# A two-layer adaLN kernel on one core: where the attention's bulk transfers and head 0's first loads stand in the queues

## The reference

```python
q = (xn @ Wq.T + bq).reshape(b, t, h, dh)
k = (xn @ Wk.T + bk).reshape(b, t, h, dh)
v = (xn @ Wv.T + bv).reshape(b, t, h, dh)
p = (pos_emb @ Wpos.T).reshape(2 * t - 1, h, dh)
content_score = jnp.einsum('bthd,bshd->bhts', q + u_bias, k)
pos_score = jnp.einsum('bthd,phd->bhtp', q + v_bias, p)
pos_score = _rel_shift(pos_score)
score = (content_score + pos_score) / math.sqrt(dh)
attn = jax.nn.softmax(score, axis=-1)
```

## Time and profile before

| | us |
|---|---|
| median of 3 runs (1020.45 to 1026.05) | 1023.15 |
| profiled execution, device time | 1029.01 |
| its span, first to last instruction | 1027.1 |
| mean granted TensorE clock | 0.917 of full |

### The profile page before, as it was taken

How to read it: one execution, slowest core, us unless ns; L and a number is a source line. 1 busy time by engine, 2 the same in 40 slices (tenths; PEclk the granted TensorE clock), 3 DMA queues, 4 the chain that set the end, 5 groups by cost and what they waited for, 6 DMA issues and landing times.

```text
span 1027.1 us, 23784 instructions
## 1 busy us (share of the span) xinstructions
PE 828.7 (81%) x9611; PEld 602.8 (59%) x9611; DVE 719.5 (70%) x1458; ACT 538.3 (52%) x985; POOL 413.7 (40%) x476
## 2 busy tenths in 40 slices
PE   2493799999999999975479998999998785257773
PEld 1252577878788888764256655666665474135563
DVE  5974656555555555425778898788786688899994
ACT  3860456677667675445545556566564644313332
POOL 5444533443344334344433245344343127214444
PEclk9986699999999999986589999999999798569998
DMA  9037613333333323541000000000000000000111
GB/s 136 11 65 215 174 39 75 94 82 78 73 92 86 79 69 85 149 97 34 1 1 2 2 1 1 2 1 2 1 2 1 1 1 1 0 1 11 20 23 31
DMA packets 55289, 47.17 MB, mean 46 GB/s; under 512 B 22259, under 2 KB 44987, under 8 KB 54459
## 3 DMA queue, kind: packets, MB, share of 16 engines
q1 hardware_dynamic: 36176, 26.23, 11.1%
q0 software_dynamic: 8416, 18.85, 7.3%
q10 hardware_dynamic: 10587, 0.57, 0.7%
HBM read 30.52 MB, written 12.06 MB: 41 GB/s over the span
## 4 chain that ended last, share of the span: by engine, by line
PE 53%; DVE 27%; issue 4%; DMA 4%; POOL 4%; ACT 4%; SPq 3%; POOLq 0%; DVEq 0%; ACTq 0%
PE PS L1154 12%; PE PS L1271 6%; PE PS L1272 5%; PE PS L1273 5%; PE PS L1127 5%; PE PS L1158 5%; PE PS L1176 5%; PE PS L1129 3%; DVE HB L1948 2%; DVE XX L1554 2%; DVE XX L1560 2%; DVE AM L1545 2%; DVE ACC L1940 1%; DVE HQ L2077 1%; DVE HN L1534 1%
## 5 line engine op out<-in xcount | busy, mean ns | idle before, releaser
L1686 DVE TENSOR_REDUCE MX<-PS 128x4 f32<-128x1024 f32 x128 | 156.4, 1224 | 120.5 <-PE PS L1129 120.1
L853 ACT ACTIVATE REG<-PS 128x1024 f32<-128x1024 f32 x128 | 130.4, 1019 | 118.4 <-PE PS L1158 112.4
L1154 PE MATMUL PS<-XX,TB 96*128 96x64 f16 x2048 | 161.3, 247 | 4.6 <-issue 2.7
L673 POOL TENSOR_TENSOR HH<-HB,HH 128x512 f16<-128x512 f32 x64 | 75.6, 1182 | 173.9 <-ACT HH L904 173.9
L1154 PEld LDWEIGHTS PS<-XX,TB 96*128 96x128 f16 x2048 | 121.9, 120 | 33.9 <-issue 12.2
L934 ACT ACTIVATE SG<-PS 128x512 f32<-128x512 f32 x128 | 76.2, 595 | 112.0 <-PE PS L1273 111.7
L1948 DVE SCALAR_TENSOR_TENSOR HB<-PS,SG 128x512 f32<-128x512 f32 x128 | 87.4, 683 | 46.0 <-ACT SG L934 46.0
L1158 PE MATMUL PS<-XX,KC 97*128 97x128 f16 x1024 | 107.8, 229 | 0.0
L1271 PE MATMUL PS<-XH,XX 128*128 128x512 f16 x256 | 98.9, 386 | 9.9 <-DVE HB L1948 9.5
L1127 PE MATMUL PS<-TM,YY 64*64 64x256 f16 x1024 | 81.5, 334 | 21.8 <-DVE YY L1728 16.3
L1272 PE MATMUL PS<-XH,XX 128*128 128x512 f16 x256 | 98.4, 384 | 0.0
(11 more groups left out here) (240 smaller groups left out, 1725.0 us busy)
## 6 DMA issues: line engine op xcount, KB each, us to landing
REG<-inverse_sums POOLq DMA_DIRECT2D x60, 128.0 KB, 2.9
KC<-keys_strips SPq DMA_DIRECT2D x16, 192.0 KB
keys_strips<-REG POOLq DMA_DIRECT2D x12, 224.0 KB, 7.2
R<-in_L_attn_x SPq DMA_DIRECT2D x32, 64.0 KB, 4.3
XX<-NEG ACTq DMA_DIRECT2D x128, 1.0 KB, 2.3
R<-REG POOLq DMA_DIRECT2D x60, 32.0 KB, 2.9
queries_position<-REG POOLq DMA_DIRECT2D x2, 896.0 KB, 8.7
XX<-queries_position SPq DMA_DIRECT2D x56, 32.0 KB
```

Of the source, the lines that this page charges most:

```text
L853: A(P[jt][:, 1024 * up:1024 * up + 1024].rearrange("p (k x) -> p k x", k=2), ST[u % 2], ACT.Exp).then_inc(exp_done, 1)
L1154: mm(o_pos[:, a], TB[p][0:96, y0:y0 + 128], xp[0:96, 8 * bank + a], start=(a == 0), stop=False, skip_group_check=True)
L1686: nc.vector.tensor_reduce(MX[h % 2][:, :].rearrange("p (r a) -> p r a", r=2)[:, :, 2 * g:2 * g + 2], PS[:, bank:bank + 2, :].rearrange("p ...
```

## The change

It moves transfers and waits in three queues; no computation is added or removed.

- **Bulk of the keys at once.** POOL's 13 bulk key transfers wait for `stage` at 14 instead of for the first heads' key transfers to have landed (`khi_first`, `k_first`).
- **SP's first transfers.** The high position queries of heads 0 to 2 (`qvb_d`) go between head 0's and head 1's key strips; before, they went behind both. Head 0's dense position queries go ahead of its key operands `KC`.
- **Dense content queries of head 0 ahead of its rows.** Its 12 position-query transfers go behind the dense content queries; before, six went ahead of them.
- `maximum_keys(1)` goes behind head 1's dense queries.
- **Bulk of the position queries later.** POOL issues `qv_d` behind its widening for head 1 and waits also for head 0's first shift row (`neg_in[0]` at 64).
- `content_first` becomes a list of two semaphores; only the second is used.

```diff
@@ SP @@
+            def first_keys(h):
+                for k, part in enumerate((0, 0, 1)):
+                    sp.dma_start(k4_d[h, :, k].rearrange("w d x -> d w x"),
+                                 NAT[NAT_K + part][DH * h:DH * h + DH, :].rearrange("p (w x) -> p w x", w=4)).then_inc(k_first, 16)
             sp.wait_ge(high_done, 14)
             sp.dma_start(khi_d[first, :], NAT[NAT_K][first, :]).then_inc(khi_first, 16)
             sp.wait_ge(stage, 14)
-            for h in range(2):
-                for k, part in enumerate((0, 0, 1)):
-                    sp.dma_start(k4_d[h, :, k].rearrange("w d x -> d w x"),
-                                 NAT[NAT_K + part][DH * h:DH * h + DH, :].rearrange("p (w x) -> p w x", w=4)).then_inc(k_first, 16)
+            first_keys(0)
             sp.wait_ge(batched, 8)
             sp.dma_start(qvb_d[first, :], NQB[first, :]).then_inc(qvb_first, 16)
+            first_keys(1)
             sp.wait_ge(khi_first, 16)
             maximum_keys(0)
+            sp.wait_ge(qvb_first, 16)
+            dense_position_queries(0)
             sp.wait_ge(k_first, 16 * 6)
             key_operands(0)
-            sp.wait_ge(qvb_first, 16)
-            dense_position_queries(0)
-            sp.wait_ge(stage, 16)
-            first_position_queries(0, range(2))
             sp.wait_ge(qu_first, 16)
             dense_content_queries(0)
-            first_position_queries(0, range(2, 4))
-            maximum_keys(1)
+            first_position_queries(0, range(4))
             dense_position_queries(1)
             dense_content_queries(1)
+            maximum_keys(1)
             key_operands(1)
@@ POOL @@
-            gp.wait_ge(khi_first, 16)
-            gp.wait_ge(k_first, 16 * 6)
+            gp.wait_ge(stage, 14)
             gp.dma_start(khi_d[rest, :], NAT[NAT_K][rest, :]).then_inc(khi_out, 16)
...
-            gp.wait_ge(x_in[0], X_FIRST[0])
-            for part in range(2):
-                gp.dma_start(qv_d[2:H, part], NAT[NAT_QV + part][2 * DH:128, :]).then_inc(qv_out, 16)
             gp.wait_ge(y_dense[1], Y_FIRST[1])
...
+            gp.wait_ge(x_in[0], X_FIRST[0])
+            gp.wait_ge(neg_in[0], 64)
+            for part in range(2):
+                gp.dma_start(qv_d[2:H, part], NAT[NAT_QV + part][2 * DH:128, :]).then_inc(qv_out, 16)
```

More of the change, by code:

```diff
@@ L260, in adaln_program @@
         l_feat, stored_last = sem("l_feat"), sem("stored_last")
-        t_evac_dve, batched, content_first, position_dense = (sem(s) for s in ("t_evac_dve", "batched", "content_first", "position_dense"))
+        t_evac_dve, batched, position_dense = (sem(s) for s in ("t_evac_dve", "batched", "position_dense"))
+        content_first = [sem(f"content_first{h}") for h in range(2)]
         block = outer.enter_context(nc.Block())
@@ L594, in _, with first_content_queries @@
                                  OWN[:, j:j + 2].unsqueeze(2).to_broadcast([128, 2, T]), ALU.mult).then_inc(y_wide[1], 1)
[L595 to L599, removed]
+            gp.wait_ge(x_in[0], X_FIRST[0])
+            gp.wait_ge(neg_in[0], 64)
+            for part in range(2):
+                gp.dma_start(qv_d[2:H, part], NAT[NAT_QV + part][2 * DH:128, :]).then_inc(qv_out, 16)
+            def first_content_queries(h):
+                for w in range(4):
+                    for k, part in enumerate(PARTS):
+                        to = 24 * w + 8 * k
+                        gp.dma_start(XC[h][to:to + 8, 1024 * w:1024 * w + 1024],
+                                     NAT[NAT_QU + part][DH * h:DH * h + DH, 1024 * w:1024 * w + 1024]).then_inc(content_first[h], 16)
+            first_content_queries(1)
             for part, h in ((0, FIRST), (1, 2)):
@@ L1141, in scores @@
                     elif h == 1:
-                        pe.wait_ge(content_first, 16 * 12)
+                        pe.wait_ge(content_first[1], 16 * 12)
                 elif h == 0 and k == 2:
```

## The result

The changed kernel took 1033.28 us (median of 4 runs, 1030.99 to 1034.53) against 1021.8 us (median of 4) for the kernel before in the same comparison. The ratio is 1.0071, with a 95% interval of 1.0037 to 1.0105: slower by 3.8 to 10.7 us. The two medians alone would give 1.0112; why the ratio is smaller is not shown, but in the three later sets the kernel before has medians of 1025.58 to 1026.03 over 24 to 29 runs, and against those 1033.28 is 1.0071 to 1.0075. The forecast was 1015, faster. A second set of runs of the same kernel, further down, gave 1.0084 (1.0054 to 1.0115).

A forecast was written before the change was run, and what follows sets the result against it. TensorE was taken as the bound, 81% busy, with a 16.27 us hole before head 0's first maximum. Gains of 6.4 and 2.3 us made 8.7, capped at 8.5 by head 1's widening: 1023.15 to 1015 us, range 1010 to 1022.

The forecast's parts named there:

- The queries' bulk: POOL's bulk of position queries: issued at 106.1 us instead of 97.34, landing at 114.8 or 115.4, at no cost.
- Some 6 us of cover remain: ACT's exponential waiting for the queries' bulk: bulk lands by about 115, exponential runs about 121.3, so no stop.
- SP's chain: SP's queue up to head 0's dense content load: issued at 82.5 us, 7.5 us earlier than 89.98.
- forecast first maximum: Head 0's first maximum on TensorE: at 90.7 us instead of 97.08, a gain of 6.4 (bounds 8.4 and 1.3).
- The 8.1: Landing time in us of head 0's old dense position load under the keys' bulk, taken for the new one.
- Rival 2: The keys' bulk starves SP's chain: first maximum at 95.8 us, a gain of 1.3; time 1019 to 1022; chance 0.26.
- arbitration rule: DMA engines alternate between queue rows by packet, so SP loads under the bulk stay near low bounds: first maximum 88.7.
- POOL's start of the keys' bulk: POOL's queue: the bulk of the keys starts at 69.14 us instead of 76.42, 7.3 us earlier.
- the shift row's gain: Ahead of the first score tile: the 2.73 us wait shrinks to about 0.4, 2.3 us gained (bounds 0 and 2.7).
- the covered row transfers: Head 0's 12 row transfers on SP: end at 94.5 us, needed at 102.0, so covered by the maxima.
- the limit set by head 1's widening: POOL's widening for head 1: ends at 106.1 us, capping the gain at 8.5 us (cap 12.6 to 5.6).
- Rival 5: TensorE's clock stays low over the rest of head 0 and head 1: costs 13 us, time 1028; chance 0.06.

The follow-up runs named there:

- e3: Changed kernel with the position queries' bulk waiting also for the second half of head 0's shift row; 0.9978 of the kernel before.
- e4: Kernel before with only the position queries' bulk moved, behind the widening and the first half of head 0's shift row; 1.0114 of the kernel before.
- e9: Kernel before with only the position queries' bulk moved, behind the widening and both halves of head 0's shift row; 0.9981 of the kernel before.
- e1: Changed kernel with the position queries' bulk back ahead of POOL's widening, waiting for head 0's rows alone; 1.0015 of the kernel before.
- e2: Changed kernel with the keys' bulk waiting for the first heads' keys again; 0.9944 of the kernel before.
- e5: Kernel before with only the keys' bulk issued at once; 1.0041 of the kernel before.
- e7: Changed kernel with the keys' bulk waiting as before and the queries' bulk behind both halves of the shift row; 0.9924 of the kernel before.
- e10: e7 with head 1's dense loads put ahead of head 0's row transfers on SP; 0.9929 of the kernel before.
- e11: e10 with the keys' bulk waiting for head 0's two dense loads to have landed; 0.9961 of the kernel before.
- e12: Changed kernel run again unaltered, for a narrower interval; 1.0084 of the kernel before.

## Why the prediction was wrong, step by step

**The queries' bulk: the step that turned the sign.** The prediction moved it from 97.34 to about 106.1 (it came at 107.38) and priced only its own reader, the exponential: "Some 6 us of cover remain". That held, in e3 too. What it left out is what the transfer now lies on. It knew of the first half of the shift row, and freed it (-2.71 us, forecast -2.3), and did not go on to the second half, four more transfers some 6 us later on the same ACT queue, for which tile 4 waits: it put their cost at nothing without a reason. Shown by e4 against e9 (11.10 us of wait, absent with one wait more), by e1 and by e3: 6 to 11 us.

**SP's chain: the step that lost the gain.** The forecast first maximum hangs on the dense content load: issued at 82.5, 8.1 us after P, with 4.9 to 8.1 us for the landing of its write. It was issued 14.9 us after P, 6.8 us later, because the write alone took 14.9 us under the bulk (5.8 in e2, where the bulk starts later). Its own landing was priced fairly (5.5, measured 4.8). With the 0.8 us of the late position part that is the whole gap between the forecast 16.3 us from P to M and the measured 23.14.

The two other hops were over their bounds as well: `KC` went 12.1 us after P (upper bound 84.9, 10.5 after P), and the dense position load, taken at 84.0, 9.6 us after P, with 86.2, 11.8 after P, as the upper bound, landed 16.8 us after P, 12.3 after its issue. The 8.1 came from a load issued 0.15 us after the bulk had started; the new one was issued when the bulk had been draining for 10 us. The bound was therefore none: it was the price of one hop at the head of the bulk, used for all. SP's issues slowed as well (`KM` 3.19 us, where 1.33 was taken; 5.98 for three strips, 1.99 each, still within the 0.83 to 2.12 allowed).

Rival 2 had this mechanism, and its argument against itself (even a load that landed only after the bulk would be in time) was too weak. The bulk had mostly drained when it was forecast to: the DMA share is 1.06 in 78 to 80 us and 0.53 in 82 to 84, that is 10 to 12 us after P, where the forecast end near 84 was 9.6 after P. But the content write and the position load landed 3 to 5 us behind 84, and content load and widening still had to follow. Shown by e2 against the changed kernel: 23.14 to 16.71 us by K alone, and by e5, where K alone costs 3.9. Why a write of this size takes some 15 us beside the bulk is not shown; nor is it shown how much of the position load's 12.3 us is the bulk and how much the strips ahead of it in SP's queue. The arbitration rule of the Trainium skill ("DMA: Bandwidth & Descriptors", "Queues, rings and completion order") would have kept the hops near their quiet price; measured for the position load were 5.8 us in e2, where the bulk started 3.1 us after it, and 12.3 with the bulk beside, so here the measurement decides against the low bounds that I drew from it.

**Right, and of no use alone:** POOL's start of the keys' bulk (69.1 with P at 74.39, that is 5.3 us ahead of P; it was 5.3), the shift row's gain, the covered row transfers, and the limit set by head 1's widening. The last never applied in the changed kernel, but it does in e2 and e7, at 33.6 and 33.7 us after P, where the prediction had 31.7.

**Clock.** Rival 5, the low clock, was the only slower case, at 0.06, and it did not decide. In 98 to 121 us the granted clock is 0.50. It stayed low for longer than before (48 us against 37.5 in 75 to 145 us), but with one wait more on POOL (e9 against e4) the loss is gone, and e5 has the same 48 us without a loss from S to C.

**Open.** The times of e10 and e11 do not show the 2.75 and 3.7 us that they gain up to C. In e11, 3.1 us are given back by head 1's late row transfers (TensorE waits 2.51 us for ACT at 125.62). In e10 most of it is gone only behind the attention, in a stretch that differs by up to 5.8 us between profiles; whether the gain is real needs more runs. That the single executions of the changed kernel differ in the wait at tile 4 was seen in two profiles, not explained.

## What to carry to other kernels

When a large transfer is moved, list every small transfer that will be in flight at its new place, on all queues, with who waits for it; its own reader is the smaller half of the question. A small load behind a chain of others is worth keeping clear of a bulk even if the bulk then ends later: here the bulk of the keys at once cost 6.4 us in the new order and 3.9 in the old. Of a change in three parts, test each alone and each left out: SP's order was worth 6 us up to the first maximum with the keys' bulk where it had been, and the two moved bulks cost more than that.

## What the runs showed that was not expected

- The same 1 KB transfers took 0.6 us to issue and 1.9 us to land beside a DMA share of 0.33, and up to 3.2 us to issue and 6.3 to 9.5 to land beside one of 0.89.
- One 64 KB load (the dense position queries of head 0) had three prices beside the same bulk: 7.4 to 9.1 us when issued within 0.3 us of its start (before, e4, e9), 11.7 to 13.0 us some nine to ten microseconds in (changed, e12, e1, e3), 6.5 us nineteen microseconds in (e5). The runs show the numbers and not why.
- A write issued into that bulk held its reader back for some 15 us: the content write in the changed kernel (14.9, 14.6 in e12, against 5.8 in e2) and the batched write in e5 (15.2, against 4.9 before).
- The wait for the second half was 7.1 us in one profile and 11.7 us in another of the same kernel.
- Behind the attention, the same instructions took from 574.98 to 580.77 us in the fourteen profiles: one profile says little of a difference in the whole time.
